# A pair's third turn of probabilities goes to the attend's output bank, and the rows' pieces become one stream laid out by quotas

## The reference, cut to what matters

```
x = x + conv(_gn(x))                        # groups of 8 channels, over a whole image
q, k, v = split(einsum(x, qkv_w) + qkv_b)   # 256 -> 3 * 256
a_r = pool(q) @ pool(k)                     # 49 x 49 affinities of 8 x 8 regions (7 x 7 of them)
idx = top_k(a_r, 4)                         # each region attends to its 4 best regions
attn = softmax(q_region * 256**-0.5 @ k[idx])   # 8 heads of 32, 64 queries x 256 keys
out = attn @ v[idx] + depthwise3x3(v)
out = einsum(out, out_w) + out_b
```

## Time and profile before

| | |
|---|---|
| median of three runs | 1864.13 us (1861.3 to 1864.42) |
| the profiled execution | 1867.38 us, its span 1864.6 us |
| granted TensorE clock | 0.997 of full speed |
| PE (matmuls) busy | 1700.5 us, 91% |
| DVE busy | 1531.7 us, 82% |
| ACT busy | 1405.5 us, 75% |
| POOL busy | 1045.4 us, 56% |
| instructions | 73643 |

### The profile page before, as it was taken

The page is one execution under the profiler, slowest core; times in us unless marked ns, Lnnn a source line. Parts: engine busy times, 40 slices in busy tenths (PEclk is TensorE's granted clock), DMA queues, the critical chain, the costliest instruction groups (busy, mean ns, idle before and its releaser), DMA issues.

```text
span 1864.6 us, 73643 instructions
## 1 busy us (share of the span) xinstructions
PE 1700.5 (91%) x26568; PEld 1359.1 (73%) x26568; DVE 1531.7 (82%) x2951; ACT 1405.5 (75%) x4401; POOL 1045.4 (56%) x2548
## 2 busy tenths in 40 slices
PE   5999899999899999989999899999899999999897
PEld 5877777777777777777777677777677777777676
DVE  5688888888888888888888888888788778789895
ACT  2477777787788778777787777778777778777674
POOL 3355556555565555655565555555556556566654
PEclk9999999999999999999999999999999999999999
DMA  5234334343334343433334333434343333365655
GB/s 198 73 92 130 106 114 129 103 135 118 114 112 131 100 142 109 122 112 116 116 114 127 119 113 108 128 107 140 101 120 101 108 95 120 93 204 168 211 187 190
DMA packets 164632, 234.43 MB, mean 126 GB/s; under 512 B 19232, under 2 KB 146912, under 8 KB 164272
## 3 DMA queue, kind: packets, MB, share of 16 engines
q1 hardware_dynamic: 141408, 129.71, 23.8%
q0 software_dynamic: 22864, 100.02, 16.2%
HBM read 166.80 MB, written 62.85 MB: 123 GB/s over the span
## 4 chain that ended last, share of the span: by engine, by line
PE 64%; ACT 15%; DVE 8%; issue 7%; SPq 3%; DMA 2%; POOL 1%; POOLq 0%; ACTq 0%; DVEq 0%
PE pt_bank L1192 18%; PE chunk_bank L1081 16%; PE s_bank L1175 10%; PE o_bank L1210 9%; ACT probs L671 8%; ACT probs_t L681 5%; PE chunk_bank L1095 4%; DVE neg_max L905 3%; PE o_bank L1218 3%; DVE lepe L792 2%; SPq L368 2%; PE chunk_bank L1108 1%; PE chunk_bank L1123 1%; DMA v_sel<-v_dram 1%; ACT v_band L628 1%
## 5 line engine op out<-in xcount | busy, mean ns | idle before, releaser
L671 ACT ACTIVATE probs<-s_bank,neg_max 128x256 f32<-128x256 f32 x1568 | 733.5, 483 | 252.3 <-DVE neg_max L905 252.3
L429 POOL COPY k_sel<-k_all 128x128 f32 x1568 | 391.5, 297 | 577.1 <-PE s_bank L1175 530.0
L905 DVE TENSOR_REDUCE neg_max<-s_bank 128x2 f32<-128x512 f32 x784 | 487.2, 684 | 237.5 <-PE s_bank L1175 237.4
L792 DVE SCALAR_TENSOR_TENSOR lepe<-v_band,taps,lepe 128x448 f32<-128x448 f32 x896 | 621.7, 743 | 0.0
L1081 PE MATMUL chunk_bank<-xn,wqkv 128*128 128x224 f32 x2544 | 584.5, 356 | 6.0 <-issue 3.4
L1192 PE MATMUL pt_bank<-ident,probs 128*128 128x128 f32 x3136 | 501.8, 283 | 92.0 <-ACT probs_t L681 84.7
L681 ACT COPY probs_t<-pt_bank 128x512 f32<-128x512 f32 x784 | 468.3, 597 | 111.4 <-PE pt_bank L1192 109.3
L1192 PEld LDWEIGHTS pt_bank<-ident,probs 128*128 128x128 f32 x3136 | 345.0, 141 | 266.1 <-ACT probs_t L681 234.9
L1081 PEld LDWEIGHTS chunk_bank<-xn,wqkv 128*128 128x128 f32 x2544 | 440.6, 192 | 12.2 <-issue 4.8
L441 POOL TENSOR_TENSOR lepe<-o_norm,lepe 128x128 f32<-128x128 f32 x392 | 275.1, 721 | 163.3 <-DVE o_norm L928 163.0
L671 ACT ACTIVATION_READ_ACCUMULATOR probs<-s_bank,neg_max 128x1 f32 x1568 | 334.5, 213 | 0.0
(11 more groups left out here) (78 smaller groups left out, 1197.2 us busy)
## 6 DMA issues: line engine op xcount, KB each, us to landing
v_sel<-v_dram SPq DMA_DIRECT2D x1568, 64.0 KB
xn<-x_dram POOLq DMA_DIRECT2D x56, 448.0 KB, 4.7
v_dram<-v_stage SPq DMA_DIRECT2D x112, 224.0 KB
resid<-x_dram POOLq DMA_DIRECT2D x31, 448.0 KB, 4.2
out_dram<-resid POOLq DMA_DIRECT2D x31, 448.0 KB, 5.5
spill<-lepe POOLq DMA_DIRECT2D x25, 448.0 KB, 3.6
xn<-spill POOLq DMA_DIRECT2D x25, 448.0 KB, 6.0
resid<-x_dram POOLq DMA_DIRECT2D x25, 224.0 KB, 3.3
```

The source lines that it names most:

```text
L429: last = pool.tensor_copy(k_sel[:, r % K_SLOTS, :, RT * j:RT * (j + 1)], k_all[:, b % 2, :, bass.ds(reg[j] * RT, RT)])
L671: act.activation(probs[:, 2 * (j % 2) + i, :], s_bank[:, u, KEYS * at:KEYS * (at + 1)], ACT.Exp, bias=neg_max[:, h % 2, col:col + 1], accu ...
L792: ins = dve.scalar_tensor_tensor(row, v_band[:, n % BANDS, k, t // 3:t // 3 + RS, t % 3:t % 3 + W], taps[:, k, t:t + 1], row, ALU.mult, AL ...
L905: dve.tensor_reduce(neg_max[:, h % 2, 2 * j:2 * j + 2], scored, AX.X, ALU.max, negate=True).then_inc(max_done, 1)
```

## The change

1. The third turn of a pair, t2, is transposed into `o_bank` where no statistics or affinities use that bank in the pair's slots (`image_work`), else into `pt_bank` as before. Into `o_bank` it waits for the normalisation of the pair before (`o_normed`) and no longer for p1. t3 then waits for p1 and no longer for p2.
2. The rows' chunks form one stream, in the order of `step_order`. F0, F1 and F2 of a pair each take 4 passes from it (a quarter counts 2, a `vt` 3), F3 the rest that is due by the pair's end; of a single region F0 takes 4 and F1 the rest. The slot tables are gone.
3. ACT copies out a chunk that ended in F0 or F1 after e2, one that ended in F2 or F3 in the next body (the first before p3, the rest after it). DVE's additions of output chunks follow the fills too: those of F0 before the first slot's row work, those of F1 and F2 between the slots' row work, those of F3 in the next body ahead of the maxima. The taps stand at the same slots in every kind of step.

```diff
+def pieces(key):
+    if key[0] == "vt":
+        return 1, 3
+    if key[0] == "rm":
+        return 2 * KC, 1
+    return QUARTERS, 2
+def quotas(h, slots):
+    if not is_duo(h) or not slots:
+        return [0] * (2 * len(slots))
+    return [4, 4, 4, 0] if len(slots) == DUO else [4, 0]
+def fill_plan():
+    order = [(s, [key for key in step_order(s) if is_row(key[1])]) for s in range(STEPS)]
+    load = [sum(pieces(key)[0] * pieces(key)[1] for key in keys) for _, keys in order]
...
+            if f == len(quota) - 1 or not enough:
+                done = slot + 1 if f % 2 else slot + 0.5
+                goal = sum(load[:int(done // NWIN)]) + (load[int(done // NWIN)] * (done % NWIN) / NWIN
+                                                        if done < STEPS * NWIN else 0)
+            else:
+                goal = spent + enough
...
+                if spent + weight / 2 > goal:
+                    break
...
+        def turn_bank(h, j):
+            return o_bank if j == 2 and not image_work(h) else pt_bank
...
-                act.copy(probs_t[:, j, :], pt_bank[:, :]).then_inc(probs_t_evac, 1)
+                act.copy(probs_t[:, j, :], turn_bank(h, j)[:, :]).then_inc(probs_t_evac, 1)
...
             for h, slots in BODIES[1:]:
-                if slots:
-                    chunk_out(slots[0])
+                paired = len(slots) == DUO
+                left = ended(h - 1, 2) + ended(h - 1, 3) if len(BODIES[h - 1][1]) == DUO else ended(h - 1, 1)
+                for key in left[:1]:
+                    chunk_out(*key)
                 if is_duo(h - 1):
                     probs_t_out(h - 1, turns_of(h - 1) - 1)
+                for key in left[1:]:
+                    chunk_out(*key)
                 exp(h, 0)
                 exp(h, 1)
                 probs_t_out(h, 0)
-                for slot in slots[1:]:
-                    chunk_out(slot)
-                if is_duo(h) and turns_of(h) == 2 * DUO:
...
+                if is_duo(h) and paired:
                     exp(h, 2)
+                    for key in ended(h, 0) + ended(h, 1):
+                        chunk_out(*key)
                     probs_t_out(h, 1)
                     exp(h, 3)
                     probs_t_out(h, 2)
...
             for h, slots in BODIES[1:]:
+                paired = len(slots) == DUO
                 if is_duo(h - 1):
                     invert(h - 1)
                     spread(h - 1)
+                if len(BODIES[h - 1][1]) == DUO:
+                    sums_out(h - 1, 3)
...
+                if is_duo(h) or paired:
+                    sums_out(h, 0)
+                    row_part(slots[0])
+                    if paired:
+                        sums_out(h, 1)
+                        sums_out(h, 2)
+                        row_part(slots[1])
...
-                if t:
+                bank = turn_bank(h, j)
+                if bank is o_bank:
+                    pe.wait_ge(o_normed, h)
+                elif j and turn_bank(h, j - 1) is o_bank:
+                    pe.wait_ge(probs_t_evac, t - 1)
+                elif t:
                     pe.wait_ge(probs_t_evac, t)
...
-            def early_part(slot):
...
+            def fill(h, f):
+                for (kind, n, k), first, last in PLAN[h][f]:
...
-                turn = 0
-                for slot in slots:
-                    early_part(slot)
+                for i, slot in enumerate(slots):
+                    fill(h, 2 * i)
                     if is_duo(h):
-                        turn_probs(h, turn)
+                        turn_probs(h, 2 * i)
                     image_part(slot)
-                    late_part(slot)
+                    fill(h, 2 * i + 1)
                     if is_duo(h):
-                        turn_probs(h, turn + 1)
-                    turn += 2
+                        turn_probs(h, 2 * i + 1)
```

More of the change, by code:

```diff
@@ L158, in step_order, with ended @@
     return late[:3] + [o0, o1, q0, q1] + late[3:]
+def pieces(key):
[11 more added lines that the diff above has]
+    load = [sum(pieces(key)[0] * pieces(key)[1] for key in keys) for _, keys in order]
+    stream = [(key, i) for _, keys in order for key in keys for i in range(pieces(key)[0])]
+    at, spent, plan = 0, 0, []
+    for h, slots in BODIES:
+        places = []
+        quota = quotas(h, slots)
+        for f, enough in enumerate(quota):
+            slot = slots[f // 2]
+            if f == len(quota) - 1 or not enough:
[4 more added lines that the diff above has]
+                goal = spent + enough
+            place = []
+            while at < len(stream):
+                key, i = stream[at]
+                weight = pieces(key)[1]
+                if spent + weight / 2 > goal:
+                    break
+                if place and place[-1][0] == key:
+                    place[-1] = (key, place[-1][1], i + 1)
+                else:
+                    place.append((key, i, i + 1))
+                spent += weight
+                at += 1
+            places.append(place)
+        plan.append(places)
+    if at < len(stream):
+        raise ValueError("chunks are left over")
+    return plan
+PLAN = fill_plan()
+def ended(h, f):
+    if not 0 <= h < len(PLAN) or f >= len(PLAN[h]):
+        return []
+    return [key for key, _, last in PLAN[h][f] if last == pieces(key)[0]]
 def chunk_places():
@@ L274, in side, with image_work @@
             return o_bank[:, at:at + n]
+        def image_work(h):
+            for slot in BODIES[h][1]:
+                s, rc = divmod(slot, NWIN)
+                if s % NWIN == LAST and is_row(s + STAT_LEAD) and rc in (1, 3):
+                    return True
+                if step_kind(s) == "first" and rc == 5:
+                    return True
+            return False
+        def turn_bank(h, j):
+            return o_bank if j == 2 and not image_work(h) else pt_bank
         late_x = k_all[:, 0, :, :].rearrange("p k t -> p (k t)").rearrange("p (i r) -> p i r", r=ROW)
@@ L757, in _ @@
                 probs_t_out(h, 0)
-                for slot in slots[1:]:
-                    chunk_out(slot)
-                if is_duo(h) and turns_of(h) == 2 * DUO:
+                if is_duo(h) and not paired:
+                    for key in ended(h, 0):
+                        chunk_out(*key)
+                if is_duo(h) and paired:
                     exp(h, 2)
+                    for key in ended(h, 0) + ended(h, 1):
+                        chunk_out(*key)
                     probs_t_out(h, 1)
@@ L764, in _ @@
                     probs_t_out(h, 2)
+                if not is_duo(h):
+                    for f in range(2 * len(slots)):
+                        if paired and f >= 2:
+                            break
+                        for key in ended(h, f):
+                            chunk_out(*key)
         @block.vector
@@ L1064, in _ @@
+                if is_duo(h) or paired:
[5 more added lines that the diff above has]
+                        row_part(slots[1])
+                else:
+                    for f in range(2 * len(slots)):
+                        sums_out(h, f)
+                        if f % 2:
+                            row_part(slots[f // 2])
         @block.tensor
@@ L1191, in turn_probs @@
                         at = P * (CH * i + c)
-                        ins = pe.transpose(pt_bank[:, at:at + P], probs[:, 2 * (j % 2) + i, P * c:P * (c + 1)],
+                        ins = pe.transpose(bank[:, at:at + P], probs[:, 2 * (j % 2) + i, P * c:P * (c + 1)],
                                            ident[:])
@@ new lines, in fill @@
+            def fill(h, f):
+                for (kind, n, k), first, last in PLAN[h][f]:
+                    if kind == "out":
+                        project_out(n, k, first, last)
+                    elif kind == "late":
+                        project_late(n, first, last)
+                    elif kind == "vt":
+                        turn_v(n, k)
+                    elif kind == "rm":
+                        region_means(n // NWIN, first, last)
+                    else:
+                        project(kind, n, k, first, last)
```

314 lines of the change are left out of this document (68 added, 246 removed).

## The result

The changed kernel takes 1809.07 us in the median of four runs (1805.92 to 1821.42), the kernel before 1862.72 beside it: a ratio of 0.9725 with a 95% interval of 0.9683 to 0.9767. Faster, as forecast, but by 54 us where I had put 106; 1809 lies just outside the range. The profiled execution is the longest of the four, 1821.42, with a span of 1819.6. The same program ran once more for the experiments: 1809.88 us, 0.9693 (0.9665 to 0.972), span 1809.2.

A forecast was written before the change was run, and what follows sets the result against it. It took a once-a-pair loop between engines, with p2 holding up t3, as the bound. Gains of 93, 8 and 5 us made 106 off 1867.4: 1761, less 3.3 for the median, 1758; range 1735 to 1808.

The forecast's parts named there:

- The third turn's bank: t2 changes bank, so t3 no longer stands behind p2: 0.60 us off ACT's loop, 7.81 becomes 7.21.
- The fills and the stall in F2: PE's steady pairs take 7.42 to 8.12 us; the later chunk copy stalls F2 0.5 us in three of seven.
- the seven pairs: Two steps of the steady part: 62.58 us before, forecast 57.4, 0.74 less a pair.
- DVE: DVE's work per steady pair: 8.86 us with two additions and five taps, 8.35 with six taps, the others 7.0 to 7.4.
- The sum: Each pair takes its longest loop; 93 us from middle pairs, 8 from other pairs, 5 from the tail: 106 us.
- the other six pairs of an image: Pairs outside an image's five middle steps: put at 0.2 us gain each, 8 us in all.
- SP is the next limit: SP's DMA starts and loads need some 26.5 us a row, 7.57 a pair, allowing 0.24 of the tail's 0.60.
- (a): Rival: PE waits for chunk banks in every pair; gain 0.45 us a pair, time 1794; chance 0.24.
- the 60 that I had named: Sign of a wrong forecast: PE's chunk rows wait over 60 us in all for ACT's or DVE's copies.
- (c): Rival: slower, a chunk bank asked for twice in a pair before it is free; 1897 at 1.5 us stall; chance 0.05.
- (b): Rival: the turn's bank changes little and SP, its queue blocked by a store, takes the gain; about 1860; chance 0.04.

The follow-up runs named there:

- the run with the stream alone: Changed kernel with every third turn back in pt_bank, so only the stream, its quotas and the moved copies remain: 1837.88 us, 0.9825.
- Weight and output half alone: Changed kernel with region means counted at 2 passes a piece and the output half ahead of the queries' half in an image's first step: 1797.26 us, 0.9627.
- the last run: Changed kernel, region means counting 2, output half earlier, ACT's copies of chunks ended in F0 to F2 made earlier only where their bank is wanted: 1766.09 us, 0.9461.
- the fourth run: Changed kernel with the keys' second half ahead of the value transposes in an image's last step: 1832.18 us, 0.9816.

## Why the prediction was wrong

**The third turn's bank: right, and in the tail sized too high.** t3 no longer stands behind p2, the wait for turns went from 84.7 us to 8.0, and t2 didn't wait for `o_normed`. A clean pair of the tail gained 0.41 us, not 0.60, because F3 is then what t3 follows. That a turn costs the same in either bank was right too: a transpose takes 273 ns in the median into both. The 622 ns of the copies out of `o_bank` against 597 out of `pt_bank` are not the bank's: all of the former are p2, and p2 took 0.62 us out of `pt_bank` as well (the earlier trace rows at 1779.07, and 622 ns in the mean of the run with the stream alone).

**The fills and the stall in F2: right for the steady part.** I gave the seven pairs 7.8, 8.1, 8.9, 8.25, 7.8, 7.8 and 8.4 us; their medians are 7.92, 8.16, 8.96, 8.50, 7.92, 7.92 and 8.47. The late copy stalls F2 as worked out, by 0.50 us in the pair of 8.96 and 0.46 in that of 8.50; those are two pairs, where I had counted three. In the seventh, DVE's addition holds PE for 0.16 us, not 0.4; another 0.24 is a turn's wait for a copy.

**DVE: sized too high, and two numbers that came out by luck.** I put the pairs of 8.9 and 8.4 on DVE's work. With the copies ahead of e2 they take 8.53 and 8.18 with the same work on DVE, less than the 8.86 and 8.35 that I had worked out for it. So 0.4 of the first was PE's stall, and what I took for DVE's period was not one.

**The sum: here it failed.** The 18 middle pairs of images 2 to 7 gave 72.7 us of 80. But the term for the other six pairs of an image, 0.2 us each, was a guess: I had worked out no fill of theirs. They were to give 8 us and lost 24.5, a miss of 33 out of 51 (106 less 55). I had checked banks for F2 and, in one steady pair, for F3 and DVE, and took the copies left for the next body as free ("beside PE's scores"). At the start of an image the means' pieces, counted at less than half their time, push the chunks on, so that an output chunk ends in F3 and its neighbours want its bank in the same fill. Weight and output half alone bring the first four pairs back to 188.6, with 8.4 us moved on to number 4; the last run has pairs 0 to 4 at 242.2, where they took 246.1 before the change and 263.9 with it. The 0.5 us that number 0 lost is still there in the last run (6.28, from 5.43), and no run tests its cause. Another 10 us are the first image: its middle steps all have two output halves, so its pairs aren't the seven that I multiplied by seven images. The runs show late copies and additions under F3 in four of its pairs (9.55, 9.36, each twice; 5 of the 10 us by the medians of their places, 8.47 and 7.92), and the last run took 0.8 to 0.9 off each of the 9.36; the pairs of 9.55 are left.

**SP is the next limit: not reached at this period.** In the tail ten of the 24 pairs took 7.40 us, under the 7.57 that I had worked out for SP, but the tail's mean is 8.3, and in the whole span SP still waits 176.5 us for the attend. PE's attend waited for `v_sel` only 5.7 us in 3 times. So SP held little back here, and whether 7.57 is its limit wasn't tested. The Trainium skill, "DMA: Bandwidth & Descriptors", section "Issuing engines are not separate DMA queues", has the time that a sequencer takes to initiate a DMA as usually small relative to the DMA itself. That SP was no limit here doesn't confirm the rule: SP's starts still take 6.81 us for eight in the tail pair's row,

```profile
1787.44 6.81 SPq L441 DMA_DIRECT2D v_sel<-v_dram  x8
```

which is 0.85 each, and the fourth run shows that a store made late in this queue costs a pair some 3 us.

**The rivals.** (a) gave 1794, nearer than my forecast, but by another way: PE's waits for chunk banks in the steady pairs stayed at three in seven, and the larger ones of the whole span (15.1, 10.4, 6.7, 4.8, 3.5 and 3.0 us) make 43.5. Another 7.0 us, in 14 waits, the profile puts down to POOL's `lepe`; these are the stalls of the pairs of 8.96, which went when the copy was moved, so they are the bank's too. Together that is 50.5, still under the 60 that I had named. (c), a bank asked for twice in a pair, is what happens at the image's start; I had priced it for the steady part alone, where it doesn't occur. (b) didn't show.

## What to carry to other kernels

When chunks in two banks are laid out by quotas, write down for every fill which chunk it starts, who frees that bank and where that stands on its engine; do it for the edges of the loop as well as for its steady part, since four pairs in 25 took back nearly all that the new layout of the fills gave. A copy's best place is not one place: ahead of the work that waits if its bank is wanted next, behind it if not. And multiply a measured stretch only by the stretches that have the same steps in them.

## What the hardware showed besides

**The clock behind a gap.** Behind a gap of 3.79 us on PE its granted clock stood at the lower of its two levels (0.50 of 2.4 GHz, so 1.2); before the gap PE had been busy for 7.54 of 8.00 us at 1.00. The profiled execution after, in stretches: columns are the stretch, its length, the busy time of PE, PEld, DVE, ACT and POOL, the granted clock, the DMA share and GB/s.

```profile
1290.00:1298.00 8.00, 7.54 (x114) 6.04 (x106) 6.52 (x13) 7.38 (x23) 4.80 (x12) 1.00 0.57 155
1302.40:1304.00 1.60, 1.55 (x10) 1.34 (x10) 0.42 (x1) 0.00 (x0) 0.00 (x0) 0.50 0.38 129
1306.00:1308.00 2.00, 2.00 (x15) 1.69 (x14) 2.00 (x4) 2.00 (x7) 0.93 (x1) 1.00 0.27 80
...
1203.10:1206.30 3.20, 3.20 (x50) 1.80 (x52) 0.07 (x1) 1.56 (x3) 0.77 (x4) 0.50 0.02 5
1420.60:1424.00 3.40, 3.40 (x108) 2.68 (x106) 1.56 (x3) 2.40 (x7) 1.86 (x8) 1.00 0.14 51
```

The last two stretches stand behind number 3's wait of 1.74 us in the sixth and in the seventh image: the clock had fallen behind the first and not behind the second. Numbers 3 and 4 took 11.57 and 8.92 us in the sixth image, 11.06 and 7.92 in the seventh. So a wait for a bank can cost more than its own length, here by 1.5 us, and such a gap doesn't always bring it. In the gap of 3.79 us PE stood still, in the middle of an attend, for a reason that the profile doesn't name:

```profile
1302.45 0.43 PE L1258 MATMUL o_bank<-probs_t,v_sel 128*32 128x64 f32 x6 [3.79 <-issue]
...
1303.30 1.70 PE L1124 MATMUL chunk_bank<-xn,wqkv 128*128 128x224 f32 x4
...
1305.53 0.92 PE L1124 MATMUL chunk_bank<-xn,wqkv 128*128 128x224 f32 x4
```

Four rows of the same kind take 1.70 us behind the gap and 0.92 two microseconds later.

**Gaps without a named reason.** PE's waits that are put down to "issue" sum to 26.8 us in this trace and to 26.3 in the kernel before. The DMA packets of the trace point at one cause. From 100 us on there are 22 such gaps of more than 0.3 us, and in all but the last a 16 KB packet of the DMA queue q8, which the page lists as an instruction queue, ended 1.1 to 1.7 us before PE went on; such packets come about every 8 us, so chance would put one there for about one gap in ten. In the kernel before that holds for 27 of 28 gaps. It looks as if PE waited for its instructions to be loaded; no run here tests that. Their sum is not the same in every program: in the run with the stream alone it was 9.5 us.
